# A transformer block on one core: the first head turns and divisions of two stages moved into the attentions before them, and the second slot's turn put between the first slot's gate and up products

## What is computed

```python
h = level_emb[levels(x)] * 0.15
h = h + attn_rel(layernorm(h))             # 16 heads of 16
X = layernorm(h)
X = X + softmax(q k^T / 4) v @ wo          # q, k, v from rmsnorm(X)
h2 = rmsnorm(X)
logits = h2 @ router_w                     # 8 experts, best 2
out = h + X + swiglu_shared(h2) + sum over the best 2 of w_e * swiglu_e(h2)
```

## Time and profile before

| what | value |
|---|---|
| runs, us | 773.08, 768.56, 771.84; median 771.84 |
| profiled execution | 769.5 us, span 767.7 |
| PE busy | 735.8 us, 96% of the span |
| weight loads (PEld) | 568.0 us, 74% |
| DVE, ACT, POOL busy | 452.9, 354.3, 192.1 us |
| chain that ended last | PE 38%, DMA 1%, all else under 1% |
| mean granted clock of PE | 0.996 of 2.4 GHz |

### The profile page before, as it was taken

The page is one execution under the profiler, slowest core; times in us unless marked ns, Lnnn a source line. Parts: engine busy times, 40 slices in busy tenths (PEclk is TensorE's granted clock), DMA queues, the critical chain, the costliest instruction groups (busy, mean ns, idle before and its releaser), DMA issues. The chain is left out here.

```text
span 767.7 us, 19039 instructions
## 1 busy us (share of the span) xinstructions
PE 735.8 (96%) x7243; PEld 568.0 (74%) x7244; DVE 452.9 (59%) x1098; ACT 354.3 (46%) x596; POOL 192.1 (25%) x294
## 2 busy tenths in 40 slices
PE   5899999999999998999998999999999999999998
PEld 2677777777668876455544874558999999999997
DVE  7777676776636555999972866512444444444442
ACT  2677777777624453577664213101433333333331
POOL 5500000000003332333320540465123222222222
PEclk9999999999999999999999989999999999999999
DMA  4500000000012445444464901124332323232322
GB/s 164 211 3 2 3 3 3 2 3 3 3 49 59 115 138 165 124 129 119 123 248 156 367 21 30 64 78 138 90 49 46 50 42 54 41 55 41 55 36 48
DMA packets 71393, 59.99 MB, mean 78 GB/s; under 512 B 7632, under 2 KB 62752, under 8 KB 71328
## 3 DMA queue, kind: packets, MB, share of 16 engines
q1 hardware_dynamic: 62896, 48.63, 20.4%
q0 software_dynamic: 7152, 9.38, 7.3%
q10 hardware_dynamic: 1280, 1.08, 0.4%
HBM read 35.78 MB, written 23.22 MB: 77 GB/s over the span
## 5 line engine op out<-in xcount | busy, mean ns | idle before, releaser
L1462 POOL DMA_INDIRECT out<-ex_Y,ex_to x39 | 60.6, 1553 | 167.6 <-DVE ex_Y L1776 164.6
L611 ACT ACTIVATE la_PT<-ps 128x512 f32<-128x512 f32 x128 | 69.5, 594 | 46.5 <-PE ps L512 46.1
L1176 DVE TENSOR_REDUCE fa_m<-ps 128x2 bf16<-128x512 f32 x128 | 84.2, 683 | 6.7 <-PE ps L1045 5.5
L1722 DVE TENSOR_TENSOR ex_hT<-ps,ex_sl 128x512 f32<-128x512 f32 x39 | 27.0, 692 | 99.5 <-PE ps L1547 99.5
L1146 ACT ACTIVATE fa_PT<-ps 128x1024 f32<-128x1024 f32 x64 | 65.4, 1024 | 39.9 <-PE ps L1060 39.7
L1547 PEld LDWEIGHTS ps<-ex_xT,V 128*128 128x128 f32 x640 | 74.5, 192 | 1.5 <-ACT ex_xT L1605 0.5
L1547 PE MATMUL ps<-ex_xT,V 128*128 128x128 f32 x640 | 74.8, 275 | 0.3 <-ACT ex_xT L1605 0.3
L1554 PE MATMUL ps<-WD,ex_hT 128*128 x312 | 73.8, 379 | 0.0
L1547 PEld LDWEIGHTS ps<-ex_xT,XS 128*128 128x128 f32 x608 | 70.8, 192 | 0.9
L1547 PE MATMUL ps<-ex_xT,XS 128*128 128x128 f32 x608 | 71.0, 275 | 0.0
L630 DVE TENSOR_TENSOR la_SM<-ps,la_SA 128x512 bf16<-128x512 f32 x64 | 44.2, 691 | 36.2 <-PE ps L498 18.6
(11 more groups left out here) (260 smaller groups left out, 1407.2 us busy)
## 6 DMA issues: line engine op xcount, KB each, us to landing
QK<-qk_parts SPq DMA_DIRECT2D x192, 64.0 KB, 2.3
qk_parts<-pj_parts SPq DMA_DIRECT2D x16, 384.0 KB, 2.8
expert_in<-zfill SPq DMA_DIRECT2D x1, 5070.0 KB, 16.9
ex_XR<-expert_in SPq DMA_DIRECT2D x39, 130.0 KB, 2.1
WG<-in_e_gate SPq DMA_DIRECT2D x8, 512.0 KB, 6.8
WU<-in_e_up SPq DMA_DIRECT2D x8, 512.0 KB, 10.4
WD<-in_e_down SPq DMA_DIRECT2D x8, 512.0 KB, 10.0
out<-HS SPq DMA_DIRECT2D x3, 512.0 KB, 4.1
```

What stands on the lines that cost most here:

```text
L611: nc.scalar.activation(PT[:, n // 2 % 2, jh, n % 2], ps[:, 2 * (n % 2) + jh], ACT.Exp, scale=QK_SCALE).then_inc(s_exp[jh], 1)
L1176: nc.vector.reduce_max(m[:, b % 2, grp, 2 * k:2 * k + 2], ps[:, h % 2].rearrange("p (f j) -> p f j", f=2), AX.X).then_inc(s_max, 1)
L1462: nc.gpsimd.indirect_dma_start(out=outs, out_offset=bass.IndirectOffsetOnAxis(ap=to[:, n:n + 1], axis=0), in_=Y[:, n], in_offset=None, com ...
```

## The change

`route`'s buffers for the division and its three small weight tiles become kept buffers, made ahead of `full_attention`; `project`'s are made ahead of `level_attention`. SP loads `wo`, `w2` and `rw` in `full_attention`, ahead of `WG`. The first `pe_turn_rows` and the first division of `project` move into `level_attention` (banks 6 and 7, PE ahead of `weigh_late`, with two of the five spins left), the second `pe_turn_rows` takes the place of its last three spins, and the second division opens `project`. The first `pe_turn_rows` of `route` moves behind the weighing of step 59 of `full_attention`, its division behind a copy of DVE's; the second turn stands at the end of that stage, its division opens `route`. The spins of `route` are set anew. In `experts` the five spins ahead of the slots go, and `turn_x(1)` stands between the gate and up products of slot 0.

```diff
--- before.py
+++ after.py
@@ -150,10 +150,18 @@
                     g.QT = g.QKT[:, 0]
                     g.ACP = lo("ACP", [P, NG, L3], BF16)
                     g.VT = lo("VT", [P, H, PADV], F32)
+                    g.pj = Shared()
+                    g.pj.AT, g.pj.rec = lo("pj_AT", [P, GT, D], F32), lo("pj_rec", [P, GT * H], F32)
+                    g.pj.rows, g.pj.recip, g.pj.at, g.pj.att, g.pj.attc = (sem("pj_" + n) for n in ("rows", "recip", "at", "att", "attc"))
                     tables(nc, g, a)
                     level_attention(nc, g)
                     project(nc, g, a)
                 g.WG = kept_right("WG", [P, E, DC, F])
+                g.rt = Shared()
+                g.rt.AT, g.rt.rec = kept_right("rt_AT", [P, 2, GT, D]), kept_right("rt_rec", [P, GT * H])
+                g.rt.W, g.rt.w2, g.rt.rw = kept_right("rt_W", [P, DC, D]), kept_right("rt_w2", [P, D]), kept_right("rt_rw", [P, DC, E])
+                g.rt.rows, g.rt.recip, g.rt.at, g.rt.att, g.rt.attc = (sem("rt_" + n) for n in ("rows", "recip", "at", "att", "attc"))
+                g.rt.s_in = sem("rt_in")
                 full_attention(nc, g, a)
             g.WU, g.WD = kept_right("WU", [P, E, DC, F]), kept_right("WD", [P, E, FC, D])
             g.SG, g.SU, g.SD = kept_right("SG", [P, DC, F]), kept_right("SU", [P, DC, F]), kept_right("SD", [P, FC, D])
@@ -575,10 +583,11 @@
                         make_unit(n + FIRST)
                 for jh in range(2):
                     sum_levels(N // 2 - 1, jh)
-                spin(nc, g, 4, 5)
+                pe_turn_rows(nc, pe, g, g.pj, 0, 6)
+                spin(nc, g, 4, 2)
                 for b in range(BP):
                     weigh_late(b)
-                spin(nc, g, 4, 3)
+                pe_turn_rows(nc, pe, g, g.pj, 1, 6)
 
             @block.scalar
             def _(act):
@@ -652,6 +661,7 @@
                     if n + FIRST < UNITS:
                         keep_unit(n + FIRST)
                 keep_sums(CHUNKS - 1)
+                dve_divide_heads(nc, dve, g, g.pj, 0, 6)
                 for b in (0, 2):
                     dve.wait_ge(s_end[0], b // 2 + 1)
                     t = ((LATE // 2) * BP + b) * 2 + LATE % 2
@@ -663,13 +673,13 @@
 GC = GT * P
 
-def pe_turn_rows(nc, pe, g, s, i):
+def pe_turn_rows(nc, pe, g, s, i, bank=0):
 
     if not first(i):
         pe.wait_ge(s.at, i)
     for k in range(GT):
         for grp in range(NG):
-            last = nc.tensor.transpose(g.ps[:, k, grp * P:(grp + 1) * P], g.OT[:, i * GT + k, grp], g.identF[:])
+            last = nc.tensor.transpose(g.ps[:, bank + k, grp * P:(grp + 1) * P], g.OT[:, i * GT + k, grp], g.identF[:])
     last.then_inc(s.rows, 1)
 
 
@@ -692,12 +702,12 @@
     nc.scalar.activation(s.ATT[:], g.ps[:, 2].rearrange("p (c t) -> p c t", c=DC), ACT.Copy).then_inc(s.attc, 1)
 
 
-def dve_divide_heads(nc, dve, g, s, i):
+def dve_divide_heads(nc, dve, g, s, i, bank=0):
 
     dve.wait_ge(s.rows, i + 1)
     if not first(i):
         dve.wait_ge(s.at, i)
-    rows = g.ps[:, 0:GT].rearrange("p k (h d) -> p (k h) d", d=PADV)
+    rows = g.ps[:, bank:bank + GT].rearrange("p k (h d) -> p (k h) d", d=PADV)
     nc.vector.reciprocal(s.rec[:], rows[:, :, DK]).then_inc(s.recip, 1)
     dve.wait_ge(s.recip, i + 1)
     if not first(i):
@@ -706,14 +716,18 @@
                             s.rec[:].unsqueeze(2).to_broadcast([P, GT * H, DK]), ALU.mult).then_inc(s.at, 1)
 
 
-def head_buffers(g, c, nc, tag, n=1):
-
-    def sb(n, sh):
-        return c.enter_context(nc.sbuf_tensor(tag + n, sh, F32))
-    s = Shared()
-    s.AT, s.ATT, s.rec = sb("AT", [P, GT, D] if n == 1 else [P, n, GT, D]), sb("ATT", [P, DC, GC]), sb("rec", [P, GT * H])
-    s.rows, s.recip, s.at, s.att, s.attc = (g.sem(tag + n) for n in ("rows", "recip", "at", "att", "attc"))
-    return s
+def dve_divide_ahead(nc, dve, g, s, i):
+
+    dve.wait_ge(s.rows, i + 1)
+    if i:
+        dve.wait_ge(s.at, i)
+    rows = g.ps[:, 0:GT].rearrange("p k (h d) -> p (k h) d", d=PADV)
+    nc.vector.reciprocal(s.rec[:], rows[:, :, DK]).then_inc(s.recip, 1)
+    dve.wait_ge(s.recip, i + 1)
+    if i >= 2:
+        dve.wait_ge(s.att, i - 1)
+    nc.vector.tensor_tensor(s.AT[:, i % 2].rearrange("p k (h d) -> p (k h) d", d=DK), rows[:, :, 0:DK],
+                            s.rec[:].unsqueeze(2).to_broadcast([P, GT * H, DK]), ALU.mult).then_inc(s.at, 1)
 
 
 def project(nc, g, a):
@@ -729,7 +743,8 @@
     with ExitStack() as c:
         def sb(n, sh, dt):
             return c.enter_context(nc.sbuf_tensor("pj_" + n, sh, dt))
-        s = head_buffers(g, c, nc, "pj_")
+        s = g.pj
+        s.ATT = sb("ATT", [P, DC, GC], F32)
         st, mv, half = sb("st", [P, GT, 6], F32), sb("mv", [P, GT, 8], F32), sb("half", [P, GT], F32)
         hn, hT = sb("hn", [P, GT, D], F32), sb("hT", [P, DC, GC], F32)
         w1 = sb("w1", [P, D], F32)
@@ -818,13 +833,10 @@
                             last = mm(ps[:, 7, k * D:(k + 1) * D], hT[:, cc, k * P:(k + 1) * P], W[:, 2, cc], start=cc == 0, stop=cc == DC - 1)
                     last.then_inc(s_v, 1)
 
-                for i in range(2):
-                    pe_turn_rows(nc, pe, g, s, i)
-                    if i == 1:
-                        output(0)
-                    else:
-                        spin(nc, g, 7, 5)
-                    pe_turn_att(nc, pe, g, s, i)
+                pe_turn_att(nc, pe, g, s, 0)
+                spin(nc, g, 4, 3)
+                output(0)
+                pe_turn_att(nc, pe, g, s, 1)
                 pe.wait_ge(s_moved, 64)
 
                 def trip(t, ahead):
@@ -945,8 +957,7 @@
                 for n in range(2):
                     V.memset(r1[0:1, n, 0:1], 0.0).then_inc(s_r1[n], 1)
                     dve.wait_ge(s_r1[n], 1)
-                for i in range(2):
-                    dve_divide_heads(nc, dve, g, s, i)
+                dve_divide_heads(nc, dve, g, s, 1, 6)
                 moments(0)
                 layer_norm(0)
                 dve.wait_ge(s_moved, 64)
@@ -1026,6 +1037,8 @@
                     if u >= 2 * RB:
                         sp.wait_ge(s_lg, (u - 2 * RB + 1) * UP)
                     load_packed(g, sp, u)
+                for o, i in ((g.rt.W, a["wo"]), (g.rt.w2, a["w2"]), (g.rt.rw, a["rw"])):
+                    sp.dma_start(o[:], i).then_inc(g.rt.s_in, 16)
                 for e in range(E):
                     sp.dma_start(g.WG[:, e], a["e_gate"][e].rearrange("(c p) f -> p c f", p=P)).then_inc(g.s_w, 16)
 
@@ -1090,7 +1103,11 @@
                         scores(ahead + 1)
                     if x >= 2:
                         weigh(x // 2 - 1, (x % 2,))
+                    if x == PAIRS - 5:
+                        pe.wait_ge(s_max, B * H)
+                        pe_turn_rows(nc, pe, g, g.rt, 0)
                 weigh(GROUPS - 1, (0, 1))
+                pe_turn_rows(nc, pe, g, g.rt, 1)
 
             @block.gpsimd
             def _(pool):
@@ -1182,27 +1199,27 @@
                 turn(GROUPS - 1)
                 for y in range(B * H // HG - 5, GROUPS, 2):
                     keep_out(y)
+                    if y == GROUPS - 5:
+                        dve_divide_ahead(nc, dve, g, g.rt, 0)
 
 
 def route(nc, g, a):
 
 
     sem, ps = g.sem, g.ps
-    (s_in, s_h, s_x2, s_var, s_r2, s_hn, s_ht, s_htc, s_lg, s_lgk, s_dv, s_half, s_kept, s_res) = (
-        sem("rt_" + n) for n in "in h x2 var r2 hn ht htc logits lkept dve half kept residual".split())
+    (s_h, s_x2, s_var, s_r2, s_hn, s_ht, s_htc, s_lg, s_lgk, s_dv, s_half, s_kept, s_res) = (
+        sem("rt_" + n) for n in "h x2 var r2 hn ht htc logits lkept dve half kept residual".split())
     with ExitStack() as c:
         def sb(n, sh, dt):
             return c.enter_context(nc.sbuf_tensor("rt_" + n, sh, dt))
-        s = head_buffers(g, c, nc, "rt_", 2)
+        s, s_in, W, w2, rw = g.rt, g.rt.s_in, g.rt.W, g.rt.w2, g.rt.rw
+        s.ATT = sb("ATT", [P, DC, GC], F32)
         st, mv, half = sb("st", [P, GT, 6], F32), sb("mv", [P, GT, 6], F32), sb("half", [P, GT], F32)
         X2 = sb("X2", [P, 2, GT, D], F32)
         hn = sb("hn", [P, GT, D], F32)
-        w2, W, rw = sb("w2", [P, D], F32), sb("W", [P, DC, D], F32), sb("rw", [P, DC, E], F32)
         with nc.Block() as block:
             @block.sync
             def _(sp):
-                for o, i in ((W, a["wo"]), (w2, a["w2"]), (rw, a["rw"])):
-                    sp.dma_start(o[:], i).then_inc(s_in, 16)
                 for o, i in ((g.SG, "sh_gate"), (g.SU, "sh_up"), (g.SD, "sh_down")):
                     sp.dma_start(o[:], a[i].rearrange("(c p) f -> p c f", p=P)).then_inc(g.s_sw, 16)
                 for e in range(E):
@@ -1259,19 +1276,17 @@
                             last = mm(ps[:, 5, k * E:(k + 1) * E], g.H2T[:, i, cc, k * P:(k + 1) * P], rw[:, cc], start=cc == 0, stop=cc == DC - 1)
                     last.then_inc(s_lg, 1)
 
-                pe_turn_rows(nc, pe, g, s, 0)
-                pe_turn_rows(nc, pe, g, s, 1)
```

(39 more changed lines are left out.)

## The result

The changed kernel takes **762.12 us**, median of 8 runs (760.77 to 765.89), against 769.39 for the kernel before, median of 8 runs beside it (766.55 to 773.08). The ratio is 0.9911, with a 95% interval of 0.9889 to 0.9933: faster by 6.85 us by the ratio (7.27 by the two medians), within 5.2 and 8.5.

What follows compares the result with a forecast made beforehand. It took PE to bound experts and project, and a fixed DVE-PE chain to bound route. Terms 1.1 + 2.3 + 1.6 + 0.85 = 5.85 off the 771.84 median gave 766.0 us, range 763.0 to 770.5.

Steps and rivals of the forecast that it cites:

- The base: Whole kernel: savings taken from the median of runs, 771.84, though the profiled execution was 769.5.
- A: level_attention into project: moved turns and division start project's work earlier, bounded by the weights' landing; 1.1 us.
- 0 if they land 1.1 later still: Start of project: no gain if the weight DMAs land 1.1 us later still.
- B: full_attention into route: moved turns and division bring the first output product earlier, with 0.3 off for row DMAs; 2.3 us.
- a delay of the last rows is covered: End of full_attention: late row DMAs are hidden by the 1.06 already paid for the turn at step 59.
- C: Last trip of route: spins in two PE waits hold the clock at 2.4 GHz; 1.6 us.
- 0.2 if the clock falls all the same: Last trip of route: gain of only 0.2 us if the clock still falls.
- minus 1.7 if it falls later and into: End of route: loss of 1.7 us if the clock falls later, into the first 3.4 us of experts.
- D: First slots of experts: five spins go and one turn moves between gate and up; 0.85 us.
- slower rival: Clock falls in A, B and D alike: +4.2 us, 776.0; chance of two or three falls 0.07.
- Absorbed by DMAs: Starts of project and route: weights and row DMAs take -1.1 and -1.1, giving 768.2; chance 0.12.
- C gives nothing: End of route: clock falls there anyway or later, giving 767.6 to 769.3; chance 0.17.

Runs made afterwards that it cites:

- e1: Changed kernel with project's first two turns and divisions back in project, with the old 13 spins: 763.97 us, ratio to before 0.9947.
- e4: Changed kernel with the eight gate-weight loads moved behind the other weights in route: 763.21 us, ratio to before 0.9934.
- e9: Changed kernel unaltered, run again with five rounds on another chip: 762.59 us, ratio to before 0.9916.
- e12: Changed kernel with gate loads late in route and nine spins for three in route's last trip: 761.31 us, ratio to before 0.9895.
- e10: Changed kernel with the spins of route's last two trips as before: 762.89 us, ratio to before 0.9919.
- e7: Changed kernel with project's weights loaded in level_attention: 768.97 us, one run.
- e3: Changed kernel with the three small loads (wo, w2, router weights) back at the start of route: 764.50 us, ratio to before 0.9952.
- e2: Changed kernel with route's turns and divisions back at its start, small loads still early: 766.55 us, ratio to before 0.9977.
- e11: Changed kernel with experts' five spins and two turns ahead of the gate products as before: 764.67 us, ratio to before 0.9929.
- e8: Changed kernel unaltered, run again on another chip for a second profile: 765.61 us, one run.
- e6: Changed kernel with gate loads late in route and nine spins for three in its last trip: 764.11 us, ratio to before 0.9890.
- e5: Changed kernel with nine spins for three ahead of route's last normed turn: 764.52 us, ratio to before 0.9893.

## Why the prediction missed low, step by step

**The base.** This is the step that failed, and the larger part of the miss of 3.9: the sum of 5.85 was put on 771.84, the median of three runs; eight runs give 769.39, and the 34 and 22 beside e1 to e4 and e9 to e12 give 768.9 and 768.8. From 769.39 the same sum gives 763.5, inside the range and within the interval of what was measured (5.2 to 8.5). I had seen that the profiled execution lay 2.3 under that median and let only the sentence on the range's low end carry it; the sum in that execution's terms, 763.65, was the better centre. The runs of the kernel before lie around 767.4 and 770.9 by their mean clock (the table above), so a median of three falls among them by chance. Which clocks the three had is not on record.

**A, 1.1 forecast.** It was 1.3 to 1.8. The block started 5.49 after the sums (5.50 forecast), and PE then waits for the weights, as worked out. Those land 3.15 after their issue in the changed profile and up to 3.79 in the others (e10), around the 3.5 taken. What was mis-sized stands behind them: "from the turn of rows at 224.99 to the end of the ten spins at 230.26 take 5.27" measured 5.04 to the normed turn, and the 1.49 from that turn to the query product shrank to 1.28 in e9 and 1.29 in e12, which the sum did not look for. e7 shows the limit of it: with no weight wait at all nothing more comes. "0 if they land 1.1 later still" never happened.

**B, 2.3 forecast.** The start gained 3.76 against some 3.66 in the sum, the turn at step 59 cost 0.93 against 1.06, so 2.83 for 2.6. The step that failed in this part is the 0.3 taken for the loads ahead of the row DMAs. Not their place sets that wait: with them ahead the wait was 0.13 in the changed profile, against some 1.45 before, and 1.7 in e1; without them it was 2.2 in e3. The cause is the gate loads, which both kernels have and e4 takes away. The bounds of nothing to 1.4 were drawn around the wrong load and left out a gain. That "a delay of the last rows is covered" by the inserted turn holds in some executions only: the changed profile's 10.79 against e2's 10.70 shows it covered, while 12.39 in e1 shows the delay and the turn added.

**C, 1.6 forecast.** Right in size where the clock holds against the profile before (11.32 - 9.58 = 1.74; the sum's own parts, 0.7 and 1.0, make 1.7), and the two exceptions the text names both occur: "0.2 if the clock falls all the same" (0.26, in the changed profile, e2 and e11) and "minus 1.7 if it falls later and into" experts (minus 2.1 in e7 and e9, minus 2.7 with the 0.6 that lies in D). Of the nine profiles with the new spins, four held the clock, three fell briefly, two fell long: (4 x 1.74 + 3 x 0.26 - 2 x 2.7) / 9 = 0.3 against that profile, and e10 against e9 measured 0.3 by the medians. What failed is taking one value for a thing that has three, and giving the two bad ones together 0.17, and taking one profile's fall for what the kernel before always pays. Two and three spins are too few: the 1.36 behind them stay empty. Nine are enough in every profile that had them, three of three, and in all 18 runs by their mean clock.

**D, 0.85 forecast.** 0.87 in the pair, 0.86 by e11. The moved turn waited for nothing, as worked out.

**The rivals.** The clock fell at neither of the new starts, in none of the 14 profiles (1.00 from 212 to 225 and from 405 to 418). The table by stretch of the changed kernel (the clock is the third figure from the end) has it at 1.00 where transposes open them:

```profile
212.00:218.90 6.90, 6.29 (x162) 4.68 (x162) 3.12 (x5) 1.97 (x4) 0.00 (x0) 1.00 0.01 2
218.90:223.40 4.50, 3.93 (x21) 2.70 (x21) 1.34 (x5) 1.60 (x4) 0.10 (x1) 1.00 0.59 204
410.00:412.30 2.30, 2.23 (x16) 1.65 (x17) 1.11 (x3) 0.60 (x1) 0.10 (x1) 1.00 0.49 42
```

So the slower rival had no place to begin, with 13 spins of A, 9 of B and 5 of D cut to 5, 3 and none. The rule of the Trainium skill (TensorE: Matmul & The Clock Gate, Part 4: PE-mode transpose), that transposes don't count as activity in the way matmuls do, is not refuted by this, as matmuls stand between them; it made no difference of time here. "Absorbed by DMAs" was half right as a place and wrong in sign. "C gives nothing" is close to what the average shows, and it didn't decide, since A and B were larger than forecast.

Summed with what was measured: A 1.6, B 2.8, C 0.3, D 0.9, together 5.6 without the row waits, which by the estimate above gave 1.3 more in the profiled pair. How much they give on average is open, as of the kernel before there is one profile, and so is the average of C. The 6.85 measured lie between 5.6 and 6.9. So the sum of 5.85 lies within what was measured, partly by luck: C came out 1.3 too high, and A, B and the row waits made up for it.

## What to carry to other kernels

Work moved from a stage's start into the stage ahead pays by the serial rounds that it removes (3.76 here) less at most its full length where the engines are paced (0.93, and 0.09 where ACT was behind anyway), so price both, and move with it every load that the earlier start will meet (1.55). Fill all of a PE wait that stands near the end of a stage, not part of it: three spins for a wait of 2.2 us left the clock to chance and the next stage's products to pay, nine cost nothing that shows and took most of the spread between runs away (5.9 to 1.4 with the gate loads moved as well). And forecast from the profiled execution, or from several runs, when the few times shown spread over more than the effect.

## What the runs showed of the hardware that was not expected

- The granted clock at one place differs between executions of the same program: 1.00 at route's end in e8, 0.52 for 3.5 us in the changed profile, half for some 10 us in e9. In all five profiles in which it fell with the new spins (changed, e2, e7, e9, e11) it did so behind the 1.36 us without PE work ahead of the last turn, between at once (e9) and some 2.5 us later. The same 1.36 stood in e1, e3, e4 and e8, and the clock held: such a gap went with a fall in five of nine executions.
- Small DMAs queued while 4.2 MB of gate weights were under way went with 0.1 to 2.2 us more in the steps by execution, and with none where those loads came later (e4, e6, e12).
- On the chip of e5 to e8, TensorE stood for 2.3 us with no cause but issue in the middle of dense products, in all four profiles. That chip's before is 3.7 longer as well (772.6 against 768.9), but no profile of it was taken there, so that the hole makes that difference is not shown. Why it comes is open.
